# Attention passes of a macaron block: part sums on TensorE in the inverse, projections amid the routing's gates, the set-up's order, and one GpSimd product in two

## The reference

```python
x = x + 0.5 * ffn(layernorm(x))        # 8 experts, the top 2 of each row
x = x + attention(layernorm(x))        # x: 4 x 1024 x 256
x = x + 0.5 * ffn(layernorm(x))

def attention(x):                      # 8 heads of 32
    q, k, v = silu(x @ Wq), silu(x @ Wk), silu(x @ Wv)
    log_f = log_sigmoid(x @ Wf1 @ Wf2)
    beta = sigmoid(x @ Wbeta) * 2.0
    k = l2norm(k); k_ = -beta[..., None] * k
    # two steps per token; S is 32 x 32 per head
    # gk = (log_f, 0), a = (k_ * exp(log_f), k_), b = (k, k), kk = (0, k), vv = (0, v)
    #   bS = b . S;  S = exp(gk) * S + a (x) bS + kk (x) vv;  o = q . S (second step)
    y = out * sigmoid(x @ Wog1 @ Wog2)
    return (rms_norm_per_head(y) * norm_w) @ Wo
```

## Time and profile before

| | us |
|---|---|
| median of 3 runs | 1971.96 (1968.42 to 1979.21) |
| the profiled execution | 1968.42 |
| its span, first to last instruction | 1966.6 |
| TensorE busy | 1525.7 (78%) |
| VectorE busy | 1165.4 (59%) |
| ScalarE busy | 780.1 (40%) |
| GpSimd busy | 755.4 (38%) |

### The profile page before, as it was taken

How to read it: one execution, slowest core, us unless ns; L and a number is a source line. 1 busy time by engine, 2 the same in 40 slices (tenths; PEclk the granted TensorE clock), 3 DMA queues, 4 the chain that set the end, 5 groups by cost and what they waited for, 6 DMA issues and landing times. The chain is left out here.

```text
span 1966.6 us, 68546 instructions
## 1 busy us (share of the span) xinstructions
PE 1525.7 (78%) x26124; PEld 1291.1 (66%) x26125; DVE 1165.4 (59%) x3492; ACT 780.1 (40%) x1805; POOL 755.4 (38%) x912
## 2 busy tenths in 40 slices
PE   5499999998656478555886647776577799999995
PEld 5499999997235365343753525545365799999994
DVE  7546444443287777767777696767956346444442
ACT  1243333332466235562345643356433243333331
POOL 2555322222075251572413725228344123522221
PEclk9999999999778598786687967878757899999998
DMA  9553322222101000010000001000100653333224
GB/s 302 182 158 86 73 48 48 48 48 38 54 7 47 22 21 22 6 46 25 22 22 4 24 27 38 17 10 12 41 12 11 217 161 60 84 68 49 47 48 109
DMA packets 84242, 116.31 MB, mean 59 GB/s; under 512 B 12952, under 2 KB 74464, under 8 KB 82016
## 3 DMA queue, kind: packets, MB, share of 16 engines
q1 hardware_dynamic: 56224, 76.27, 12.2%
q0 software_dynamic: 27360, 37.80, 10.7%
q10 hardware_dynamic: 544, 0.86, 0.1%
HBM read 64.87 MB, written 54.21 MB: 61 GB/s over the span
## 5 line engine op out<-in xcount | busy, mean ns | idle before, releaser
L1059 POOL DMA_INDIRECT x<-ffn_yout,ffn_place x142 | 222.2, 1565 | 532.3 <-DVE ffn_yout L991 449.0
L997 DVE TENSOR_TENSOR ffn_inner<-ffn_inner,ffn_bank 128x512 f32<-128x512 f32 x142 | 97.5, 687 | 354.7 <-PE ffn_bank L871 352.3
L871 PE MATMUL ffn_bank<-ffn_tileT,ffn_gate_now 128*128 128x128 f32 x2272 | 280.2, 277 | 0.0
L871 PE MATMUL ffn_bank<-ffn_tileT,ffn_up_now 128*128 128x128 f32 x2272 | 278.3, 276 | 0.0
L881 PE MATMUL ffn_bank<-ffn_w,ffn_inner 128*128 x1136 | 268.9, 380 | 1.7 <-DVE ffn_yout L991 1.7
L871 PEld LDWEIGHTS ffn_bank<-ffn_tileT,ffn_gate_now 128*128 128x128 f32 x2272 | 268.4, 194 | 0.1
L952 ACT ACTIVATE ffn_inner<-ffn_bank 128x512 f32<-128x512 f32 x142 | 84.8, 597 | 459.9 <-PE ffn_bank L871 459.8
L871 PEld LDWEIGHTS ffn_bank<-ffn_tileT,ffn_up_now 128*128 128x128 f32 x2272 | 266.7, 193 | 0.0
L881 PEld LDWEIGHTS ffn_bank<-ffn_w,ffn_inner 128*128 128x128 f32 x1136 | 205.0, 190 | 24.4 <-issue 2.5
L814 ACT COPY ffn_gate_now<-ffn_w 128x1024 f32 x142 | 148.4, 1045 | 29.1 <-issue 21.9
L814 DVE COPY ffn_up_now<-ffn_w 128x1024 f32 x142 | 98.9, 696 | 52.6 <-issue 42.4
(11 more groups left out here) (493 smaller groups left out, 3114.0 us busy)
## 6 DMA issues: line engine op xcount, KB each, us to landing
ffn_w<-in_w1t_dram SPq DMA_DIRECT2D x16, 1024.0 KB, 5.4
ffn_tile<-xs SPq DMA_DIRECT2D x122, 130.0 KB, 2.1
ffn_w<-in_w2t_dram SPq DMA_DIRECT2D x16, 512.0 KB, 6.5
ffn_x<-in_x_dram SPq DMA_DIRECT2D x16, 256.0 KB, 5.8
x<-ffn_x SPq DMA_DIRECT2D x16, 256.0 KB, 5.7
pass_xa<-x SPq DMA_DIRECT2D x12, 256.0 KB, 3.2
pass_xr<-x SPq DMA_DIRECT2D x12, 256.0 KB, 2.6
x<-pass_xr SPq DMA_DIRECT2D x12, 256.0 KB, 2.2
```

The source lines that it names most:

```text
L871: t = pe.matmul(bank[:, i * P:(i + 1) * P], half_now[half][b][:, k, i * P:(i + 1) * P], rowsT[b][:, k * P:(k + 1) * P], start=(k == 0), st ...
L997: dve.tensor_tensor(inner[b][:, :], inner[b][:, :], p_u[b][:, :], ALU.mult).then_inc(s_act, 1)
L1059: pool.indirect_dma_start(total, bass.IndirectOffsetOnAxis(ap=place[b][:, 0:1], axis=0), yout[b][:, :], None, compute_op=ALU.add).then_inc ...
```

## The change

Five edits:

- The last of GpSimd's products (L1730, 128x512) becomes two of 128x256, one for each column of the pair.
- In the last doubling (size 16) VectorE keeps the multiplications, in a ring of seven buffers, and adds only neighbouring pairs from the fourth term on; TensorE adds the ten terms left through the identity in PSUM (z in banks 2 and 3, x in banks 0 and 1). The v and gate projections move ahead of these sums, behind `back` 3; `back` 4 to 9 are set among them; ScalarE's copies of the inverse's last quarters read PSUM.
- With routing, job 0 and the first matmul of job 1 go between the gates; jobs 2 to 4 come before the counts; the eight jobs use seven banks with other waits; the squares' banks and waits change.
- In the set-up wq, wv, wo are loaded once the rows have landed.
- `setup.vector_end` goes from the end of VectorE's begin stage to before `log_f`.

```diff
@@ gate_tensor
+            if spare is not None:
+                spare(i)
         gate(GT - 1)
@@ setup_scalar
+            for h in range(2):
+                act.wait_ge(s_x[h], 16 * BATCH // 2)
             for dst, src in ((wq, "wq"), (wv, "wv"), (wo, "wo")):
@@ between
-    SQUARES = [psum[i] for i in (3, 2, 0, 1)]
+    BANKS = [psum[i] for i in ((2, 4, 5, 0, 1, 6, 2, 0) if routes else (0, 1, 2, 0, 1, 2, 0, 1))]
+    SQUARES = [psum[i] for i in ((1, 2, 0, 3) if routes else (3, 2, 0, 1))]
...
                 def job(j):
-                    t, w, g, c = JOBS[j]
-                    if j >= 3:
+                    if routes and j in (1, 2, 5):
+                        pe.wait_ge(s_lf, 1 + j // 2)
+                    elif routes and j >= 6:
+                        pe.wait_ge(s_ev, 3 * j - 17)
+                    elif j >= 3 and not routes:
                         pe.wait_ge(s_ev, j - 2)
...
+                def between_gates(i):
+                    if i == 1 or i == 3:
+                        part(0, i // 2)
+                    elif i == 5:
+                        pe.wait_ge(s_lf, 1)
+                        part(1, 0)
...
-                    r.gate_tensor(pe, 0)
+                    r.gate_tensor(pe, 0, spare=between_gates)
+                    part(1, 1)
+                    for j in range(2, 5):
+                        job(j)
+                    r.count_tensor(pe, 0)
...
+                        if routes:
+                            pe.wait_ge(s_ev, (5, 7, 8, 8)[j])
+                        else:
+                            pe.wait_ge(s_ev, min(j + 5, 8))
-                        if j == 0 and ends:
+                        if j == 3 and routes:
                             pe.wait_ge(r.s_rows, 1)
@@ between, vector
                 elif begins:
+                    if setup is not None:
+                        setup.vector_end(dve)
                     for j in range(4):
                         log_f(j)
@@ decays_and_triangles, gpsimd
-                        pool.tensor_tensor(out[:, :, 8:12].rearrange("p n (a s) -> p n a s", s=2), planes([[0, 2]]),
-                                           late2.unsqueeze(3).to_broadcast([P, NB, 2, 2]), ALU.mult).then_inc(s_pr, 1)
+                        for s, first in ((0, kf2), (1, two(k, c))):
+                            i = pool.tensor_tensor(out[:, :, 8:12].rearrange("p n (a s) -> p n a s", s=2)[:, :, :, s],
+                                                   first[:, :, 0:1].to_broadcast([P, NB, 2]), late2, ALU.mult)
+                        i.then_inc(s_pr, 1)
@@ invert
+    SMALL = sum(2 * (2 * m - 1) for m in SIZES[:-1])
+    TERMS = (0, 1, 2, 3, 5, 7, 9, 11, 15, 13)
+    FORMED = (1, 2, 3, 7, 10, 13, 16, 19, 21, 22)
+    PRODUCT, PARTS = FORMED[-1], len(TERMS)
...
+        for p, one, two in ((0, zterm, zpair), (1, xterm, xpair)):
+            if p > 0:
+                eng.wait_ge(s_acc, PARTS)
+            for x in range(CT):
+                if 7 <= x <= 10:
+                    eng.wait_ge(s_acc, PARTS * p + x - 6)
+                elif x in (12, 14):
+                    eng.wait_ge(s_acc, PARTS * p + x // 2 - 1)
+                step(one(x))
+                if x in (5, 7, 9, 11, 13):
+                    step(two(x - 2))
+            step(two(CT - 3))
...
+            def total(p, y):
+                x = TERMS[y]
+                pe.wait_ge(s_inv, SMALL + PRODUCT * p + FORMED[y])
+                if p == 0:
+                    for half in range(2):
+                        heads = slice(half * HQ // 2, (half + 1) * HQ // 2)
+                        t = pe.matmul(z_sum[:, heads, :, 0:CT - x], ident[:, :], term(x)[:, heads, :, 0:CT - x],
+                                      start=(y == 0), stop=(y == PARTS - 1), skip_group_check=True)
...
+            for n in range(4):
+                back(n)
+            for j, (t, g, c) in enumerate(VALUES):
...
+            pe.wait_ge(s_vale, len(VALUES))
+            for p in range(2):
+                for y in range(PARTS):
+                    total(p, y)
+                    if (p, y) == (0, 3):
+                        pe.wait_ge(s_tc, 2)
+                        back(4)
+                    elif (p, y) == (0, 5):
+                        back(5)
...
+                    elif (p, y) == (1, 6):
+                        pe.wait_ge(s_tc, 3)
+                        back(8)
...
+            pe.wait_ge(s_tc, 4)
+            back(10)
+            back(11)
```

More of the change, by code:

```diff
@@ L1373, in _ @@
                 if routes:
-                    r.gate_tensor(pe, 0)
-                if begins:
-                    for j in range(4):
-                        job(j)
-                if routes:
-                    r.count_tensor(pe, 0)
-                if begins:
-                    for j in range(4, 8):
+                    r.gate_tensor(pe, 0, spare=between_gates)
[3 more added lines that the diff above has]
+                    r.count_tensor(pe, 0)
+                elif begins:
+                    for j in range(5):
+                        job(j)
+                if begins:
+                    for j in range(5, 8):
                         job(j)
@@ L1550, in _ @@
                         dve.tensor_tensor(both(kb, g, c), both(k, g, c), psum[4 + j][:, :], ALU.mult).then_inc(s_kb, 1)
-                if setup is not None:
-                    setup.vector_end(dve)
 def decays_and_triangles(nc, sb, sem, psum, s, env, last=False):
@@ L1929, in step @@
                 eng.wait_ge(s_inv, n[0] - 1)
-        for size, m in enumerate(SIZES):
+        for size, m in enumerate(SIZES[:-1]):
             if size == 0:
@@ new lines, in _ @@
+            pe.wait_ge(s_ev, GROUPS)
+            pe.wait_ge(s_aq, 3)
+            for n in range(4):
+                back(n)
+            for j, (t, g, c) in enumerate(VALUES):
+                if j < 4:
+                    pe.wait_ge(s_bke, j + 1)
+                    for kc in range(KCH):
+                        t = pe.matmul(psum[j][:, :], wv[:, kc, g * P:(g + 1) * P], xT[:, kc, c * 512:(c + 1) * 512],
+                                      start=(kc == 0), stop=(kc == KCH - 1))
+                else:
+                    pe.wait_ge(s_vale, j - 3)
+                    t = pe.matmul(psum[j % 4][:, :], wrank[RANK:2 * RANK, g * P:(g + 1) * P], fg[RANK:2 * RANK, c * 512:(c + 1) * 512], start=True, stop=True)
+                t.then_inc(s_val, 1)
@@ L2065, in _, with compact, back @@
                 i.then_inc(s_ev, 1)
-            def compact(rows, cols):
-                act.copy(tc[:, rows, :, cols], tmv[:, :, rows, cols].rearrange("p h j i -> p j h i")).then_inc(s_tc, 1)
-            for n in range(12):
-                if n == 4:
-                    act.wait_ge(s_inv, STEPS - LAST)
-                    compact(slice(0, CT), slice(0, SUB))
-                    compact(slice(CT, SUB), slice(CT, SUB))
-                if n == 8:
-                    act.preload_act_table_set("silu_and_others")
-                    for j, (t, g, c) in enumerate(VALUES):
-                        act.wait_ge(s_val, j + 1)
-                        if j < 4:
-                            act.activation(both(t, g, c), psum[j][:, :], ACT.Silu).then_inc(s_vale, 1)
-                        else:
-                            act.activation(both(t, g, c), psum[j % 4][:, :], ACT.Tanh, scale=0.5).then_inc(s_vale, 1)
-                    act.wait_ge(s_inv, STEPS - LAST // 2 + CT)
-                    compact(slice(CT, CT + CT // 2), slice(0, CT))
-                if n == 10:
-                    act.wait_ge(s_inv, STEPS)
-                    compact(slice(CT + CT // 2, SUB), slice(0, CT))
+            def compact(rows, cols, src=None):
+                src = tmv[:, :, rows, cols] if src is None else src
+                act.copy(tc[:, rows, :, cols], src.rearrange("p h j i -> p j h i")).then_inc(s_tc, 1)
+            def back(n):
                 act.wait_ge(s_bk, n + 1)
@@ L2090, in _ @@
                 act.copy(ta[:, :, :, col:col + 4].rearrange("p u c j -> p c u j"),
-                         psum[n % 8][:, :].rearrange("p (j c u) -> p c u j", j=4, c=CHAINS)).then_inc(s_bke, 1)
+                         back_bank(n)[:, :].rearrange("p (j c u) -> p c u j", j=4, c=CHAINS)).then_inc(s_bke, 1)
+            for n in range(4):
+                back(n)
+            act.preload_act_table_set("silu_and_others")
+            for j, (t, g, c) in enumerate(VALUES):
+                act.wait_ge(s_val, j + 1)
+                if j < 4:
+                    act.activation(both(t, g, c), psum[j][:, :], ACT.Silu).then_inc(s_vale, 1)
+                else:
+                    act.activation(both(t, g, c), psum[j % 4][:, :], ACT.Tanh, scale=0.5).then_inc(s_vale, 1)
+            act.wait_ge(s_inv, SMALL)
+            compact(slice(0, CT), slice(0, SUB))
+            compact(slice(CT, SUB), slice(CT, SUB))
+            for n in range(4, 8):
+                back(n)
+            act.wait_ge(s_acc, PARTS + TERMS.index(CT // 2 - 1) + 1)
```

(7 more changed lines are left out.)

86 lines of the change are left out of this document (53 added, 33 removed).

## The result

The changed kernel takes 2007.1 us (median of four runs, 2005.6 to 2007.6) beside 1974.0 for the kernel before; the ratio is 1.017, 95% interval 1.014 to 1.020. The forecast was 1941, its range ended at 1965. The profiled execution has a span of 2005.1 us, 38.5 more than before.

The account below looks back on a forecast made before the run. Bounds: VectorE in the inverse, GpSimd in decays and triangles, TensorE between passes from the gates on. Terms -9.5 - 5.5 - 10 - 4.4 = -29.4 gave 1941 us; the forecast's own range was 1930 to 1952, the overall range 1912 to 1965.

Parts of the forecast that it names:

- GpSimd's halves: Decays and triangles: L1730 as two products of 256 saves 0.30 us per chain, -9.5 us (-14 to +8).
- The inverse: Last doubling (size 16): sums moved from VectorE to TensorE, -1.4 us per pass, -5.5 us in four (-15 to +12).
- `back` 0 to 3 start at 621.82: Inverse's last doubling: TensorE's transposes start then, take 3.5 us at half clock, and the eight jobs run from 625.3.
- VectorE starts at 625.41: Inverse's first product: VectorE starts then and stalls 6.5 us before its eighth term, until TensorE takes the first at 639.3.
- ten terms 10.5: Inverse's products: TensorE adds ten terms through the identity at full clock in some 10.5 us.
- Rival C: Inverse's sums run at half clock: ten terms take 21 us, +21 a pass, total about 2030; chance 0.06.
- stands at half clock: Inverse's last doubling before the change: TensorE has little to do there and runs at half clock.
- The gates: Between passes: projections amid the gates at full clock, squares at 789.2 instead of 792.64, -3.4 per stage, -10 us in three.
- Rival B: Clock falls in the gates as today (1957), or GpSimd's halves are each dear (1958); both 1974; chance 0.18.
- Set-up: Set-up: `vector_end` moved into VectorE's idle time and wq, wv, wo loaded behind the rows, -4.4 us (-2.5 to -5.5).
- The scan: The unedited scan: hangs on TensorE's clock, taken as 0 change, scans at 72 us as before.
- Rival D: Stalls before the eighth term and at the third projection are larger; only set-up and some GpSimd gain stay: 1962 to 1972; chance 0.14.

Follow-up runs that it names:

- e12: The whole changed kernel with GpSimd's scatter begun only after ScalarE's last turned copy: 1969.4 us, 0.996 of the kernel before.
- e5: The kernel before with the inverse's edit alone and GpSimd's scatter begun only after ScalarE's last turned copy: 1981.3 us, ratio 1.004.
- e2: The changed kernel with the old inverse, so every edit but the inverse's: 1965.1 us, 0.994 of the kernel before.
- e3: The kernel before with the projections amid the gates alone: 1979.9 us, ratio 1.000.
- e1: The kernel before with the inverse's edit alone, scatter at its old place: 2027.5 us, ratio 1.025.
- e4: The kernel before with GpSimd's product in two and the set-up's edits, nothing else: 1965.1 us, ratio 0.993.
- e7: The kernel before with the eight value jobs and their evacuations moved ahead of the copy of the small blocks, VectorE untouched: 1974.9 us.
- e6: The kernel before with the inverse's edit alone, plus 32 more instructions (met waits) on ScalarE in the set-up: 2022.0 us.
- e8: The kernel before with 37 more instructions (met waits) in TensorE's part of each inverse: 1978.7 us.
- e10: The kernel before with 55 more instructions (met waits) behind VectorE's part of each inverse: 1986.7 us.
- e9: The kernel before with the inverse's edit alone, plus 9 instructions behind VectorE's part of each inverse, restoring its program's old length: 2021.7 us.
- e18: The kernel of e15 run once more, unchanged, on another chip: 1972.7 us.
- e15: The kernel before with VectorE's half of the inverse's edit alone, plus 16 instructions behind VectorE's part of each inverse: 1915.3 us.
- e11: The kernel before with the inverse's edit, scatter after the copies, and two 512-column matmuls between TensorE's last gate job and first total: 1994.6 us, ratio 1.012.

## Why the prediction was wrong, point by point

**1. GpSimd's halves: right.** -12.0 for -9.5, the pair and the chain within 0.05 us. The rule from the Trainium skill, GPSIMD Engine Reference, Performance pitfalls for Q7 kernels (half as much again per element beyond a step of 8 bytes), would have made the pair 1.9 to 2.2 us, an estimate from L1725's row, with and without its fixed 0.30 us left alone. The row says 1.55 at steps of 512 bytes: the trace doesn't agree, and the nearest row was the better guide.

**2. The inverse: wrong in its starting time and in one rate.** The mechanism of the sums held: seven buffers, a stall before the eighth term, the second product 13.4 us, 17.8 us from its start to the scan (17.5 to the stage's end forecast). Two steps failed.

The first is the wait at the start. "`back` 0 to 3 start at 621.82" and "VectorE starts at 625.41" were taken from the trace of before, and the edit's new wait on VectorE, for all 18 copied groups instead of 12, stands in the sum at nothing. In that trace it would cost nothing: the last copy is done 3.6 us before VectorE wants it. Where ScalarE pauses under the scatter the last copy comes 7 to 12 us later, the old code hides it, and the new code pays: z16 at 21.6 to 24.4 us instead of 17.7, +23.2 us over four passes, and 13.6 more in the first products (117.5 us, in e12, which is without pauses, 103.9), since VectorE has lost its distance from the value jobs. No row of before showed a pause, so its size couldn't be foreseen; that z16 now hung on ScalarE's copies, with 3.6 us to spare, could.

The second is "ten terms 10.5", all at full clock: the first three took 1.5 to 3.1 us more in the changed kernel (e5: 1.8 to 3.2). It rested on the earlier trace rows, where dense work kept 1.00, but four thin jobs stand between that work and the terms. Rival C was right on place and mechanism, with up to 3 us a pass instead of 21. (The prediction's "stands at half clock" fits TensorE in the second product of before, 0.50; in the first says 0.85.)

Without the pauses an inverse takes 61.5 us against 60.6 (e5, e12): +0.9, not -1.4, so the edit would bring nothing even then.

**3. The gates: wrong by the clock, and its price too low.** The earlier trace rows said that the gates run at 0.50 with TensorE never idle, 9.10 of 9.10. I assumed that the added products would lift the clock, and costed them at 0.86. In ten of the twelve stages of the profiled changed kernel, e2, e3 and e12 they didn't (gates of 12.4 to 13.4 us; 9.9 in the other two), and each cost 2.06 us with no slack to hide in: a step of 1.17 us is already full with transposes and gates. Rival B named this and gave +2 a stage, by 1.7 us a product; it was +4.1 against the trace of before (12.2 in three), of which some may be the stretch's own spread (73.8 to 77.8 us without this edit in e1 and e4). Even at 1.00 the gates took 9.9 us and the stage gained 0.9 (e3).

**4. Set-up: right.** -4.3 for -4.4.

**5. The scan: right in the sum** (-3.7 for 0), but a single scan ranges from 72 to 82 us over the runs, with its mean clock.

**Rival D** expected larger stalls "by a later value job" and gave 1962 to 1972 for it. The value jobs did come later; what lay outside every case was that unedited copies would pause and that the new wait would let the pauses through to VectorE. Without the pauses the sign would have held: e12 is 0.4% faster than the kernel before on the same chip, though far from the forecast's 1.6%.

**What stays open.** Shown: the pauses need the scatter beside the copies (e1 against e5, the changed kernel against e12); in the group of runs with the long first stage they come in all fourteen profiled runs that have the scatter at its old place, whatever is edited; and they delay z16 only where VectorE waits for all 18 groups. The order (e7), 32 instructions more on ScalarE (e6), 37 on TensorE (e8), 55 on VectorE (e10) and VectorE's length as before (e9, e18) neither bring them nor take them away. Open is what tells the two groups apart. Chip 13 was in the first, chips 1, 5, 6, 7 and 8 in the second, but each chip's kernels ran at one time, so chip and occasion aren't separated. The kernel before wasn't profiled in the second group, nor the changed kernel in the first; that the changed kernel would start z16 at 17.7 us there, as e15 does, is argued only. Why ScalarE pauses is open too. That it waits for its instructions would fit `issue`, and would fit that the copies of 1.9 and 2.2 us from SBUF amid the same scatter (618.7 to 622.8 us in the changed kernel) ran without a pause; it is argued only. The Trainium skill, Runtime: NRT & Kernel Launch, Instruction fetch mechanics, says that each engine's instructions are fetched ahead by a DMA queue of its own and that this is mostly hidden; no row here tells whether it was.

## What to carry to other kernels

Before a product is put "into the gaps" of a dense thin stretch, read its granted clock: at 0.50 each product costs twice, and a busy share of 9.10 in 9.10 leaves no gap. Work moved to the engine that idles must be costed at the clock that holds where it lands, and thin jobs just ahead of it are a reason to doubt full speed. A new wait isn't free because the trace shows it met in time: note how much time it has to spare, and on whom it now depends. When an unedited line slows down, look at what runs beside it (here GpSimd's scatter) and move that first; compare two kernels on one chip before a difference is put down to the code; and look for an effect where it arises (ScalarE's rows), since a mark on another engine shows it only through a wait.

## What the runs showed of the hardware that I had not expected

- ScalarE pauses of 0.7 to 6.7 us beside GpSimd's indirect DMAs, for nothing that the profile shows, in every profiled run on five chips that had the scatter there, and in neither run on a sixth; one kernel took 1915.3 and 1972.7 us.
- TensorE's granted clock fell from 1.00 to 0.50 with no idle time at all: in three of e11's four passes, at the end of four jobs of 32 rows or in the dense products of 128 rows behind them (3.10 to 3.68 us for records that take 1.98 at 1.00).
- Gates of the same code run at either level of the clock from stage to stage (9.9 or 13.4 us in one run of e3).
